# A graph-attention block on one core: head projections in three chunks, one f2 transpose for four heads, the second ffn layer as split f32r, new orders

## The reference

```python
def _gat_heads(x, adj, W, a):
    Wh = jnp.einsum('bnf,hfo->bhno', x, W)
    f1 = jnp.einsum('bhno,ho->bhn', Wh, a[:, :O])
    f2 = jnp.einsum('bhno,ho->bhn', Wh, a[:, O:])
    e = f1[:, :, :, None] + f2[:, :, None, :]
    e = jnp.where(e > 0, e, LEAKY_ALPHA * e)
    e = jnp.where(adj[None, None] > 0, e, NEG_INF)
    attn = jax.nn.softmax(e, axis=-1)
    return jnp.einsum('bhnm,bhmo->bhno', attn, Wh)
...
    h = jax.nn.elu(_gat_heads(enc_inputs, adj, W_heads, a_heads))
    h = jnp.transpose(h, (0, 2, 1, 3)).reshape(B, N, -1)
    out = _gat_heads(h, adj, W_out[None], a_out[None])[:, 0]
    out = jax.nn.elu(out)
    ffn = jnp.maximum(out @ w1 + b1, 0.0) @ w2 + b2
    y = ffn + out
...
    return (y - mu) / jnp.sqrt(var + LN_EPS) * ln_gamma + ln_beta
```

## Time and profile before

| | us |
|---|---|
| median of 3 runs | 1364.8 (1364.24 to 1365.14) |
| the profiled execution | 1362.21 |
| its span | 1360.4 |
| PE busy | 1305.1 (96%) |
| ACT busy | 1116.3 (82%) |
| DVE busy | 1095.9 (81%) |
| POOL busy | 371.1 (27%) |
| granted PE clock, mean | 0.991 |

### The profile page before, as it was taken

The page is one execution under the profiler, slowest core; times in us unless marked ns, Lnnn a source line. Parts: engine busy times, 40 slices in busy tenths (PEclk is TensorE's granted clock), DMA queues, the critical chain, the costliest instruction groups (busy, mean ns, idle before and its releaser), DMA issues.

```text
span 1360.4 us, 27728 instructions
## 1 busy us (share of the span) xinstructions
PE 1305.1 (96%) x10109; PEld 1254.3 (92%) x10109; DVE 1095.9 (81%) x2848; ACT 1116.3 (82%) x2152; POOL 371.1 (27%) x252
## 2 busy tenths in 40 slices
PE   6799999999999999999999999999999999999885
PEld 6799999999999999999999999999999999999874
DVE  5978788798878879887887978888798777877544
ACT  5889888888888988888898889889788888978642
POOL 0031231413223141322314132322323224132412
...
GB/s 178 21 74 40 17 17 49 32 49 31 40 48 17 48 32 48 33 40 48 17 48 32 40 40 40 48 32 40 17 40 48 40 42 23 32 24 48 9 32 15
DMA packets 42206, 53.32 MB, mean 39 GB/s; under 512 B 2836, under 2 KB 30808, under 8 KB 42072
## 3 DMA queue, kind: packets, MB, share of 16 engines
...
...
## 4 chain that ended last, share of the span: by engine, by line
PE 79%; DVE 10%; ACT 6%; issue 4%; DMA 1%; POOL 1%; SPq 0%; ACTq 0%; DVEq 0%; POOLq 0%
PE ps L1101 59%; PE ps L1214 8%; PE ps L1316 4%; PE ps L1280 3%; DVE arg L986 2%; DVE prob_lo L957 1%; ACT arg L785 1%; PE ps L1253 1%; PE ps L1290 1%; ACT prob_hi L791 1%; DVE arg L1012 1%; DVE st L939 1%; PE ps L1176 1%; DVE elu L1023 1%; DVE whx_lo L957 1%
## 5 line engine op out<-in xcount | busy, mean ns | idle before, releaser
L658 POOL TENSOR_TENSOR hx_lo<-elu,hx_hi 128x512 fp32r<-128x512 f32 x128 | 166.6, 1304 | 661.6 <-ACT hx_hi L815 660.4
L1101 PE MATMUL ps<-prob_hi,whx_hi 128*128 128x256 f32 x1024 | 296.0, 289 | 2.8 <-DVE prob_lo L957 2.1
L1101 PE MATMUL ps<-prob_hi,whx_lo 128*128 128x256 f32 x1024 | 289.6, 283 | 0.0
L1101 PE MATMUL ps<-prob_lo,whx_hi 128*128 128x256 f32 x1024 | 289.5, 283 | 0.0
L785 ACT ACTIVATE arg<-arg,nmax 128x512 f32<-128x512 f32 x320 | 226.9, 712 | 3.9 <-DVE nmax L997 3.7
L957 DVE TENSOR_TENSOR prob_lo<-ps,prob_hi 128x1024 fp32r<-128x1024 f32 x160 | 195.1, 1220 | 32.4 <-ACT prob_hi L791 32.1
L781 ACT ACTIVATE arg<-arg,fcol 128x512 f32<-128x512 f32 x320 | 212.3, 714 | 8.5 <-DVE gmax L986 8.4
L986 DVE CUSTOM_DVE_ANT_0 arg<-f2bc,mask 128x512 f32<-128x512 f32 x308 | 207.3, 710 | 3.6 <-PE ps L1214 3.0
L1101 PEld LDWEIGHTS ps<-prob_hi,whx_hi 128*128 128x128 f32 x1024 | 195.9, 191 | 6.5 <-DVE prob_lo L957 3.8
L1101 PEld LDWEIGHTS ps<-prob_hi,whx_lo 128*128 128x128 f32 x1024 | 196.1, 191 | 0.3
L1101 PEld LDWEIGHTS ps<-prob_lo,whx_hi 128*128 128x128 f32 x1024 | 195.9, 191 | 0.0
...
## 6 DMA issues: line engine op xcount, KB each, us to landing
f2bc<-f_rows SPq DMA_DIRECT2D x77, 256.0 KB, 3.3
xb<-in_x SPq DMA_DIRECT2D x16, 512.0 KB, 4.8
xin<-in_x SPq DMA_DIRECT2D x15, 512.0 KB, 3.9
out_x<-xb SPq DMA_DIRECT2D x15, 512.0 KB, 2.9
f_rows<-f2row SPq DMA_DIRECT2D x77, 2.0 KB
...
```

Of the source, the lines that this page charges most:

```text
L658: pool.tensor_tensor(out=hx[1][:, 2 * c.h:2 * c.h + 2, c.u * HN:(c.u + 1) * HN], in0=elu[:, c.buf, :, :], in1=hx[0][:, 2 * c.h:2 * c.h + 2 ...
L1101: i = pe.matmul(out, a, b_, start=(k == 0), stop=(k == n - 1))
```

## The change

The head weights lie in one row of 8 + 1024 columns (all f1 and f2 columns first) and are multiplied in three chunks of 344 columns: m1 is 3 chunks by 2 halves instead of 4 heads by 2 halves, 72 matmuls a batch instead of 96. Chunk 0 holds all the f1 and f2, head 0 and the first 80 columns of head 1. The evictions go by chunk. On ACT the eviction of chunk k waits until head k+1's attention of the batch before has ended. One f2turn (32 rows) serves the four heads, BACK has its own. The second ffn layer is a `product` in f32r: Relu stays in PSUM, ACT copies its high part, DVE makes the low part; w2 is split once at the start. One slot instead of two holds the spread f2. All orders are new.

```diff
-ROUND_FROM, ROUNDS = 8, 8
+ROUND_FROM, ROUNDS = 15, 7
...
+    FC = 2 * H
+    CHUNKS = 3
+    CW = (FC + H * F) // CHUNKS
...
-    F2S = 2
+    F2S = 1
...
-        w2_sb = sb("w2_sb", [P, KC, F])
+        w2w = [sb(f"w2_{s}", [P, KC, F], f32r) for s in ("hi", "lo")]
...
+        def chunk_of(h):
+
+            return (FC + (h + 1) * F - 1) // CW
...
             def f2bcast(c):
...
+                d, t = by_dma.index(head), turn_of(c.info, c.b)
                 if d >= F2S:
                     sp.wait_ge(max_made, 4 * (by_dma[d - F2S] + 1))
-                sp.wait_ge(f2_out[d % 4], 16 * (d // 4 + 1))
-                if d == 1:
-                    sp.wait_ge(s_w1, 1)
-                sp.dma_start(f2bc[:, d % F2S, :], f2_rows[d % 4].partition_broadcast(P)).then_inc(f2_spread[d % F2S], 16)
+                sp.wait_ge(f2_out[t % 4], 16 * (t // 4 + 1))
+                sp.dma_start(f2bc[:, d % F2S, :], f2_rows[c.b % 2, H if c.info == BACK else c.info].partition_broadcast(P)).then_inc(f2_spread[d % F2S], 16)
...
@@ scalar @@
             def w1_prep(c):
                 act.wait_ge(ld[LD_W1], 16)
                 act.activation(w1x[0][:, :, :], w1_st, ACT.Copy).then_inc(s_w1_hi, 1)
+                act.wait_ge(ld[LD_W2], 16)
+                act.activation(w2w[0][:, :, :], w2_st, ACT.Copy).then_inc(s_w1_hi, 1)
...
             def m1(c):
-                h, p = c.info
-                act.wait_ge(m1_done, 2 * H * c.b + 2 * h + p + 1)
+                k, p = c.info
+                act.wait_ge(m1_done, 2 * (CHUNKS * c.b + k) + p + 1)
                 if c.b > 0:
-                    wait(act, att_done, unit_number[c.b - 1, h, 1] + 1)
-                act.activation(whx[:, 2 * p:2 * p + 2, h, 0:F], pairs[c.pair][:, :, 0:F], ACT.Copy).then_inc(m1_hi, 1)
+
+                    wait(act, att_done, unit_number[c.b - 1, k + 1, 1] + 1)
+                a = FC if k == 0 else 0
+                act.activation(whx_row[0][:, 2 * p:2 * p + 2, k * CW + a - FC:(k + 1) * CW - FC], pairs[c.pair][:, :, a:CW], ACT.Copy).then_inc(m1_hi, 1)
...
-                    act.activation(midT[:, o, c.cols], ffn1_out(c, o), ACT.Relu,
-                                   bias=b1c[:, o:o + 1]).then_inc(f1_read, 1)
+                    act.activation(ffn1_out(c, o), ffn1_out(c, o), ACT.Relu, bias=b1c[:, o:o + 1]).then_inc(f1_relu, 1)
+                for o in range(KC):
+                    act.wait_ge(f1_relu, KC * (c.n - 1) + o + 1)
+                    i = act.activation(midT[0][:, o, c.cols], ffn1_out(c, o), ACT.Copy)
+                i.then_inc(mid_hi, 1)
...
@@ vector @@
             def m1(c):
...
+                a = FC if k == 0 else 0
+                cols = slice(k * CW + a - FC, (k + 1) * CW - FC)
+                i = lo(whx_row[1][:, 2 * p:2 * p + 2, cols], ps[:, :, a:CW], whx_row[0][:, 2 * p:2 * p + 2, cols])
+                if k == 0:
+                    i = dve.tensor_copy(fcol[:, c.b % 2, :, :, 2 * p:2 * p + 2].rearrange("p s h n -> p n (s h)"), ps[:, :, 0:FC])
+                i.then_inc(m1_read, 1)
...
+            def ffn1(c):
+                dve.wait_ge(mid_hi, c.n)
+                for o in range(KC):
+                    i = lo(midT[1][:, o, c.cols], ffn1_out(c, o), midT[0][:, o, c.cols])
+                i.then_inc(mid_lo, 1)
...
@@ tensor @@
             def m1(c):
...
-                    r = product(pairs[c.pair][:, i, 0:FA],
-                                [(hT[0][:, k, n * P:(n + 1) * P], hT[1][:, k, n * P:(n + 1) * P], wh[0][:, k, h, :], wh[1][:, k, h, :])
-                                 for k in range(KC)])
+                    r = product(pairs[c.pair][:, i, 0:CW],
+                                [(hT[0][:, z, n * P:(n + 1) * P], hT[1][:, z, n * P:(n + 1) * P], wh[0][:, z, cols], wh[1][:, z, cols])
+                                 for z in range(KC)])
...
             def f2turn(c):
...
-                    pe.wait_ge(m1_read, 2 * H * c.b + 2 * h + 2)
-                    column = fcol[:, h, 1, :]
+                    pe.wait_ge(m1_read, 2 * CHUNKS * c.b + 2)
+                    columns = fcol[:, c.b % 2, 1, :, :].rearrange("p h n -> p (h n)")
...
             def ffn2(c):
                 if c.b == 0:
-                    pe.wait_ge(ld[LD_W2], 16)
-                pe.wait_ge(f1_read, KC * c.n)
+                    pe.wait_ge(s_w1, 2)
+                pe.wait_ge(mid_lo, c.n)
...
-                    for k in range(KC):
-                        i = pe.matmul(y, midT[:, k, n * P:(n + 1) * P], w2_sb[:, k, :], start=(k == 0), stop=(k == KC - 1))
+                    i = product(y, [(midT[0][:, k, n * P:(n + 1) * P], midT[1][:, k, n * P:(n + 1) * P], w2w[0][:, k, :], w2w[1][:, k, :])
+                                    for k in range(KC)])
```

The orders are new on every engine. The round of PE, and the parts of the rounds of SP and DVE that the prediction follows:

```diff
 ROUND, SP
-    f2send:2@6 f2bcast:2@6 f2send:3@6 load@4 f2bcast:3@6 f2send:0@5 f2bcast:0@5 store@8 f2send:1@5 f2bcast:1@5 load_back@7
-    f2send:-1@6 f2bcast:-1@6
+    f2send:0@11 f2bcast:0@11 f2bcast:1@11 store@14 load_back@13 f2send:-1@12 f2bcast:-1@12 f2bcast:2@11 load@9 f2bcast:3@11
 ROUND, PE
-    f2turn:2@5 turn_p:2@5 m1:00@4 turn_gc@7 turn_p:3@5 m1:01@4 attend:2@5 conv_in:0@7 f2turn:3@5 conv_in:1@7 turn_p:4@6
-    attend:3@5 m1:10@4 turn_p:5@6 attend:4@6 turn_p:6@5 f2turn:0@4 attend:5@6 m1:11@4 conv@7 turn_out@6 attend:6@5 turn_p:7@5
-    turn_p:8@5 ffn1@6 f2turn:1@4 attend:7@5 attend:8@5 turn_p:9@5 m1:20@4 m1:21@4 ffn2@6 m1:30@4 attend:9@5 mix2:0@5
-    turn_p:0@4 mix2:1@5 turn_p:1@4 mix2:2@5 mix2:3@5 attend:0@4 f2turn:-1@5 m1:31@4 turn_in@3 attend:1@4
+    mix2:3@11 attend:0@10 f2turn:-1@11 turn_in@9 m1:21@10 attend:1@10 turn_p:2@10 turn_gc@12 turn_p:3@10 attend:2@10
+    conv_in:0@12 turn_p:4@11 conv_in:1@12 m1:00@9 attend:3@10 turn_p:5@11 m1:01@9 attend:4@11 attend:5@11 turn_p:6@10 conv@12
+    f2turn:0@9 turn_out@11 turn_p:7@10 attend:6@10 turn_p:8@10 ffn1@11 attend:7@10 turn_p:9@10 m1:10@9 attend:8@10 ffn2@11
+    attend:9@10 m1:11@9 turn_p:0@9 m1:20@9 mix2:0@10 mix2:1@10 mix2:2@10 turn_p:1@9
 ROUND, ACT
...
+    elu_neg:2@11 elu_exp:2@11 conv_in:0@13 hx:1@11 args:5@12 probs:4@12 conv_in:1@13 args:6@11 m1:00@10 probs:5@12 hx:2@11
+    elu_neg:3@11 elu_exp:3@11 args:7@11 hx:3@11 m1:01@10 elu_neg:4@12 elu_exp:4@12 elu_neg:5@12 elu_exp:5@12 probs:6@11
...
 ROUND, DVE
...
+    scale:0@11 m1:10@11 ffn2@13 norm_in_out@10 norm_ff@13 elu_out:9@12 rowmax:2@11 rowmax:3@11 rowmath:2@11 rinv:1@11
+    norm_ff_out@13 m1:11@11 scale:1@11 probs:0@11 rowmath:3@11 mix2:0@12 rinv:2@11 x2@13 m1:20@11 norm_gc@13 mix2:1@12
...
+    rowmax:4@12 turn_gc@13 rowmath:4@12 rowmax:5@12 rowmath:5@12 rinv:4@12 scale:4@12 probs:3@11 elu_out:2@11 conv_in:0@13
+    rowmax:6@11 rowmath:6@11 rinv:5@12 rowmax:7@11 scale:5@12 probs:4@12 conv_in:1@13 rinv:6@11 rowmath:7@11 m1:00@10
...
```

More of the change, by code:

```diff
@@ new lines @@
+    rowmath:0@3 scale:9@2 elu_out:6@2 rowmath:1@3 probs:8@2 ffn1@1 norm_in@4 probs:9@2 elu_out:7@2 rinv:0@3 rowmax:2@3
+    scale:0@3 rowmath:2@3 m1:10@3 rinv:1@3 elu_out:8@2 ffn2@1 elu_out:9@2 norm_ff@1 norm_in_out@4 rowmax:3@3 m1:11@3 scale:1@3
+    norm_ff_out@1 rowmath:3@3 probs:0@3 mix2:0@2 m1:20@3 x2@1 probs:1@3 norm_gc@1 mix2:1@2 rinv:2@3 rinv:3@3 norm_gc_out@1
+    scale:2@3 elu_out:0@3 scale:3@3 m1:21@3 turn_in@4 probs:2@3 rowmax:4@2 rowmath:4@2 elu_out:1@3 turn_gc@1 rowmax:5@2
+    rowmath:5@2 rinv:4@2 probs:3@3 scale:4@2 rinv:5@2 rowmax:6@3 elu_out:2@3 conv_in:0@1 rowmath:6@3 probs:4@2 scale:5@2
@@ L178 @@
+    probs:5@-1 elu_neg:5@-1 elu_exp:5@-1 turn_out@-1 turn_out:1@-1 ffn1@-1 ffn1:1@-1 norm_ff_out@-1 norm_ff_out:1@-1
+    norm_gc_out@-1 turn_gc@-1 norm_gc_out:1@-1 turn_gc:1@-1 conv_in:0@-1 conv_in:1@-1
     """,
     "DVE": """
[L180 to L182 removed]
@@ L232 @@
[L232 to L236 removed]
+    m1:10@-5 ffn2@-7 scale:0@-5 norm_ff@-7 elu_out:9@-6 rowmax:2@-5 norm_in_out@-4 rinv:1@-5 rowmath:2@-5 m1:11@-5 rowmax:3@-5
@@ new lines @@
+    probs:8@-2 rowmax:1@-1 rowmath:0@-1 ffn1@-3 elu_out:7@-2 rinv:0@-1 elu_out:8@-2 rowmath:1@-1 probs:9@-2 ffn2@-3 norm_ff@-3
+    m1:10@-1 scale:0@-1 elu_out:9@-2 rinv:1@-1 norm_ff_out@-3 rowmax:2@-1 m1:11@-1 rowmath:2@-1 rowmax:3@-1 x2@-3 mix2:0@-2
+    probs:0@-1 rowmath:3@-1 scale:1@-1 norm_gc@-3 rinv:2@-1 rinv:3@-1 scale:2@-1 scale:3@-1 mix2:1@-2 m1:20@-1 probs:1@-1
+    norm_gc_out@-3 elu_out:0@-1 m1:21@-1 probs:2@-1 elu_out:1@-1 rowmax:4@-2 rowmath:4@-2 turn_gc@-3 rowmax:5@-2 rowmath:5@-2
@@ new lines @@
+    rinv:4@-2 scale:4@-2 probs:3@-1 elu_out:2@-1 conv_in:0@-3 rowmax:6@-1 rinv:5@-2 rowmath:6@-1 scale:5@-2 probs:4@-2
+    rowmax:7@-1 conv_in:1@-3 probs:5@-2 rinv:6@-1 rowmath:7@-1 scale:6@-1 elu_out:3@-1 rowmax:8@-1 elu_out:4@-2 probs:6@-1
+    rowmath:8@-1 rinv:7@-1 elu_out:5@-2 scale:7@-1 conv@-3 rinv:8@-1 scale:8@-1 rowmax:9@-1 rowmath:9@-1 turn_out@-2 rinv:9@-1
+    probs:7@-1 probs:8@-1 scale:9@-1 elu_out:6@-1 ffn1@-2 elu_out:7@-1 probs:9@-1 elu_out:8@-1 ffn2@-2 norm_ff@-2 elu_out:9@-1
@@ new lines @@
+    norm_ff_out@-2 mix2:0@-1 x2@-2 norm_gc@-2 norm_gc_out@-2 mix2:1@-1 rowmax:4@-1 turn_gc@-2 rowmath:4@-1 rinv:4@-1
```

(4 more changed lines are left out.)

505 lines of the change are left out of this document (252 added, 253 removed).

## The result

The changed kernel took 1372.3 us (median of 4 runs, 1372.1 to 1375.0) where the kernel before took 1364.5 beside it: ratio 1.0067, interval 1.0055 to 1.0080. The profiled execution's span is 1370.3 us, 9.9 above that of before.

What follows compares the result with a forecast made beforehand. PE was taken to bound the middle. Savings of 9.1 + 5.3 + 1.0 = 15.4 us on PE, plus 1 from the edges, made 16.4: 1364.8 became 1348 (profiled span 1360.4 to 1344.0), range 1339 to 1359.

Steps and rivals of the forecast that it cites:

- SP's queue: Store, load_back, x_beta and power before norm_ff_out: 12 us; DVE may stand 1 to 3 us, priced at nothing.
- the edges: Prologue, tail and PE idle from 821 to 1211 us: +1 for the tail, -2 for the rest.
- What bounds the kernel: Middle, 265 to 821 us: PE never idle, so a microsecond of PE work removed is a microsecond of time.
- PE terms: The change's three savings on PE, 15.4 us in sum, for a round of 78.4.
- (1): Second ffn layer: 8 fp32 matmuls become 24 f32r, -0.57 us a batch, -9.1 over 16.
- (2): f2 transposes: 5 a batch become 2, at 0.11 us each, -0.33 a batch, -5.3 in all.
- (3): Head projections: 96 matmuls of 258 columns become 72 of 344 at 0.158 us, -0.06 a batch, -1.0 in all.
- the Trainium skill's roofline: Matmul issue gap: about 81 ns at 128 columns, 131 at 512; set aside because the trace has 120 and 234.
- Order of the round: New waits all covered: ffn2's 3.7 us by 8.5, the ffn1 pair by 2 to spare, the f2 slot by 0.7.
- rival B: m1:00's eviction waits for attend:3: a small new wait of 0.4 to 0.8 us a round, 1354 to 1360; chance 0.15.
- C: ACT reaches m1:00 one softmax late: PE stands 1.8 us a round, 1377, slower; chance 0.07.
- The chances: Whole kernel against before: faster 0.88, within 0.2% (2.7 us) 0.05, slower 0.07.

Runs made afterwards that it cites:

- ffn2_only: Kernel before, own orders and chunks, with one slot for spread f2 and the second ffn layer as split f32r: 1420.8 us, ratio 1.0425.
- four2: Changed kernel's work in the orders of before, with four narrow chunks and VectorE's ffn1 behind scale:9 in batches up to 7: 1415.8 us in one run.
- combo_first: combo with m1:11 and m1:20 of batch 0, probs:2 and probs:3 of batch 1 and m1:00 of batch 2 moved earlier: 1369.5 us.
- sp_mid: Changed kernel with store and load_back ahead of f2bcast:1 in SP's queue in the seven middle batches: 1369.1 us, ratio 1.0041.
- combo: Changed kernel with turn_p:2 ahead of attend:1 and, on SP, store and load_back ahead of f2bcast:1 (batch 13's sends also earlier): 1362.4 us, ratio 0.9993.

## Why the prediction was wrong

The forecast for the profiled execution's span was 1344.0 us, and 1370.3 was measured. Of the 26.3 between them 11.3 are new waits from batch 3 to 10, forecast as none (seven rounds at some 1.04, and the waits behind SP's queue), 15.3 are the edges (+14.3 where -1 was forecast), and 0.3 came back on PE's work. In steps of the prediction:

- **What bounds the kernel.** Right as a reading of before, wrong as a rule. That a microsecond of PE work taken out of a batch is a microsecond of time holds only while the waits of PE stay covered by that same work. By ffn2_only and four2 some covers were under 0.6 us, which a chain that is all PE doesn't show. The chain before says that no wait is open, and nothing on how far each is from opening.
- **PE terms.** (1) -0.57 a batch: the row fell by 0.62 in the trace; undoing it costs 6.2 us, 9.1 forecast. (2) 0.11 held for the turn that serves four heads (L1263). It has 16 rows, four heads by four tiles (128*16 in the trace), and not the 32 that I wrote. (3) 1.89 to 1.90 us for twelve of 344 columns, 0.158 each, as worked out. Sum 15.7 for 15.4. Where the prediction sets 120 and 234 ns beside the Trainium skill's roofline for 128 and 512 columns, 120 is the price at 256; at 128 the rows have 109 (0.87 for eight transposes), which leaves the comparison as it came out.
- **Order of the round: the step that failed.** I gave the covers of ffn2, the ffn1 pair and the slot, which held in the round (the ffn1 pair failed once, by 1.8 us before m1:10 of batch 13), and none for attend:2, though the change takes m1:00 and m1:01 (3 us of filler) away from it. The wait is 1.04 us a round: between rival B's 0.4 to 0.8 and C's 1.8, at neither's place. B had the cause half right: m1:00 now carries columns of head 1 and its eviction waits for attend:3, so in its old place it would hold a PSUM pair. combo_first shows what that costs: m1:00 in that gap in batch 1 made a wait of 2.97 us one of 5.95.
- **SP's queue.** The chain of store, load_back, x_beta and the power was seen, at 12 us (it took 13.5 in the profile, from 408.1 to 421.6 us) and 1 to 3 us of VectorE, and priced at nothing. That the sends behind it would be late as well wasn't seen. By the medians of sp_mid and combo the order of that queue is worth 3 to 5 us; by the pitches 2.6 of it are clearly the edit's.
- **The edges: by size the larger miss.** -1 forecast, +14.3 measured: +10.1 up to batch 3 and +4.2 behind batch 10. I had priced operations added and removed there, not the rewritten order. Up to batch 2 the table above gives that order 1.5 to 2 us, the half clock 2.5, and leaves 2.5 open; most of the rest is the 3.0 us of work saved up to batch 3, which don't show in the time. Behind batch 10, the waits of 1.8 and 1.38 us are the only ones followed. How the order's share splits between the width of the chunks and the placement of steps wasn't told apart.
- **The chances.** 0.07 for slower, with 15 us of sure saving against orders that were new on five engines, was too low: 1.04 us a round alone took the round's saving back (79.53 against 79.40), which is where C puts the turn; the 8 us beyond it come from SP's queue and the edges.
